# Reordering inside a slot of an attention stage: the score maxima, GpSimd's half of a remainder, and two small edits of the first slots

## The chip, the cores and the metric

The kernel runs on one core of a Trainium2 chip. The metric is the device time of one execution in microseconds; the median of several runs is compared. The engines are TensorE (PE in the rows), VectorE (DVE), ScalarE (ACT) and GpSimd (POOL); SyncE (SP) issues the DMAs. Each engine works through its own queue of instructions in the order in which they are written, and they meet at semaphores.

## The reference

```python
# x (4, 2048, 512), ctx (4, 77, 512); Wq, Wo (512, 512); 16 heads of 32
xn = layernorm(x)
Q, K, V = split(xn @ Wq.T), split(ctx @ Wq.T), split(ctx @ Wq.T)
attn = softmax(Q @ K.T / sqrt(32))
x = x + merge(attn @ V) @ Wo.T
# feed-forward, activations and weights fake-quantized to int8
xq = fake_quant(layernorm(x), clip_x)
h = fake_quant(silu(xq @ qw(w_gate).T) * (xq @ qw(w_up).T), clip_down)
x = x + h @ qw(w_down).T
```

All tensors are float32. The attention part needs accuracy beyond one reduced-precision product, so most operands are kept as a high part and a remainder (hi + lo), and products are made of three terms.

## The kernel before, in words

The kernel has three stages: `attend` (to about 600 us of the span), `expand` and `contract`. The change touches only `attend`.

`attend` treats the 8192 tokens in 16 blocks of 512. A block has 4 groups of 128 feature columns (4 heads each), and one group of one block is an item: 64 items, n = 0 to 63, with `n.block = n // 4` and `n.g = n % 4`. The work is pipelined over slots k = -9 to 72. In each slot every engine handles parts of several items, and `at(k, lag)` is item k + lag. Each engine has its own `for k in SLOTS` loop; the order in which its parts are written is the order in which it executes them.

TensorE in slot k, before: scores of item k-2 (L937, with the negated maxima added by L941), denominators and attention times V of item k-3 (L888, L893, L897, L901), in slots with k % 4 == 1 a transposition of the maxima (L860), the q product of item k+4 (L961: 12 matmuls, 8 with the high part of x and 4 with its remainder), the maxima's scores of item k+3 (`maximum`, L874: 4 matmuls into the same PSUM banks `S` that the scores use), and last the output projection of item k-7 (`project`, L918, 12 matmuls). The order of waits matters here: `maximum(n)` waits for the exponentials of item n-5 and the reduction of item n-1, the scores of item k-2 for the reduction of item k+2 (`maxed`), and `project(n)` for `aT_l` of all four items of n's block, and it waits for the fourth of them already at the first item of the block.

ScalarE in slot k: exponentials of item k-2 (L569), the fp16 cast of both halves of the probabilities (L573 for `HA`, L575 for `HB`; before item 7 the first is done by VectorE at L728), logarithm and reciprocal of the denominators of item k-3 (L586, L588), the high part of x (L594), the high part of q of item k+4 (L616), a weight's int8 code (L632), and last the high part of the attention output of item k-3 into `aT` (L636), once VectorE has written `att`.

VectorE in slot k: statistics of a token tile (L680, L681), moments of the finished rows of item k-8 (L691 to L693), measuring of a weight (L646; L652 and L653 when a row of it is finished), the remainder of half `HA` of the probabilities of item k-2 (L730, `pl_a`), the scaling of q of item k+4 (L738), the reduction of the maxima's scores of item k+3 (L745), `att` of item k-3 (L752, into one buffer, so that it waits for `aT_l` of the item before), and the sum with x of item k-7 (L791).

GpSimd in slot k, before: the remainder of x (L489), the remainder of the attention output of item k-4 (L494, `aT_l`), the remainder of q (L498), the half `HB` of the remainder of the probabilities of item k-2 (L504, `pl_b`; it waits for VectorE's half of the same item), then small parts: K's remainder in slot -1 (L508), spreading K over the head mask for the next batch (L481), Wo's remainder (L519), a weight's cast (L529), and the factors of layernorm (L535 to L539).

Of the kernel before, what the change touches and what calls it, by code (L numbers as in the profile page):

```python
# [24 lines left out]
F32 = mybir.dt.float32  # L25
# [151 lines left out]
EXP_BITS, V_BITS = 11, 12  # L177
EARLY, LATE = 7, 60
V_SLOTS = (2, 3, 4, 6)
SQ = 32  # L180
STAT_LAGS = ((9, 0, TT), (8, TT, 2 * TT), (9, 2 * TT, 3 * TT), (11, 3 * TT, STEPS))

# [28 lines left out]
def attend(nc, x_t, x_k, ctxT, WqT, WoT, clip_x, clip_down, w_gate, w_up, w_down, ident, headmask, negsel,  # L211
# [8 lines left out]
    with ExitStack() as st:  # L220
# [94 lines left out]
        def at(k, lag):  # L315

            return Item(k + lag) if 0 <= k + lag < STEPS else None
# [44 lines left out]
        with nc.Block() as block:  # L362
# [108 lines left out]
            @block.gpsimd  # L471
            def _(pool):
                own = Chain(pool, own_p)
                nc.gpsimd.memset(allones[:], 1.0).then_inc(consts, 1)
                nc.gpsimd.memset(epsb[:], EPS).then_inc(consts, 1)
                nc.gpsimd.memset(mx[:], 0.0).then_inc(mx_zero, 1)
                nc.gpsimd.memset(ones[:], 1.0).then_inc(consts, 1)
                nc.gpsimd.memset(ebias[:], EXP_BITS * math.log(2.0)).then_inc(consts, 1)
                def spread_k(b, j):

                    nc.gpsimd.tensor_scalar(kbd[:, b % 2, :, j], kt[:, b, 0].bitcast(F32), hmask[:, j:j + 1], None,  # L481
                                            ALU.mult).then_inc(kbd_rdy, 1)

                for k in SLOTS:
                    for n in [n for n in (at(k, 8), at(k, 7)) if n and (n.block < 2) == (n.n == k + 8)]:
                        if n.n == 2:
                            pool.wait_ge(rs_rdy, 1)
                        pool.wait_ge(xT_h, n.n + 1)
                        nc.gpsimd.tensor_tensor(xT[:, n.par, 1, n.g], xt32[:, n.n % RINGX], xT[:, n.par, 0, n.g].bitcast(F32),  # L489
                                                ALU.subtract).then_inc(xT_l, 1)  # L490
                    if (n := at(k, -4)) and n.n < STEPS - 1:

                        pool.wait_ge(aT_h, n.n + 1)
                        nc.gpsimd.tensor_tensor(aT[:, n.par, 1, n.g], att[:], aT[:, n.par, 0, n.g].bitcast(F32),  # L494
                                                ALU.subtract).then_inc(aT_l, 1)
                    for n in [n for n in (at(k, 4), at(k, 3)) if n and (n.n <= 5) == (n.n == k + 4)]:
                        pool.wait_ge(qT_h, n.n + 1)
                        nc.gpsimd.tensor_tensor(qT[:, n.ring, 1], q32[:, n.n % 2], qT[:, n.ring, 0].bitcast(F32), ALU.subtract).then_inc(qT_l, 1)  # L498
                    if (n := at(k, -2)) and n.n < LATE:

                        pool.wait_ge(ph_b, n.n + 1)
                        pool.wait_ge(pl_a, n.n + 1)
                        after(pool, valued, n.n)
                        nc.gpsimd.tensor_tensor(pl[:, HB], pr[:, HB], ph[:, HB], ALU.subtract).then_inc(pl_b, 1)  # L504
                    if k == -1:
                        pool.wait_ge(k32_rdy, 1)
                        for g in range(GROUPS):
                            nc.gpsimd.tensor_tensor(kt[:, :, 1, g], k32[:, g].rearrange("p (b k) -> p b k", b=BATCH),  # L508
                                                    kt[:, :, 0, g].bitcast(F32), ALU.subtract).then_inc(k_lo, 1)
                    if k == -5:  # L510
                        pool.wait_ge(c_in, 16)
                        nc.gpsimd.tensor_copy(negw[:], neg[:].unsqueeze(2).to_broadcast([P, GROUPS, KEYS])).then_inc(consts, 1)
                        pool.wait_ge(mask_in, 16)
                        pool.wait_ge(k_hi, GROUPS)
                        for j in range(HG):
                            spread_k(0, j)
                    if 0 <= k < KT:
                        pool.wait_ge(wo_hi, k + 1)
                        nc.gpsimd.tensor_tensor(wo[:, 1, k], wo32[:, k], wo[:, 0, k].bitcast(F32), ALU.subtract).then_inc(wo_lo, 1)  # L519
                    b, j = k // PER + 1, k % PER - 4  # L520
                    if 0 <= j < HG and 1 <= b < BATCH:
                        after(pool, m_scored, PER * (b - 1))
                        spread_k(b, j)
                    if k == 8:
                        nc.gpsimd.tensor_copy(id16[:], id32[:])
                    if (w := weight(k - W_FIRST - 2)) and w.coded:
                        pool.wait_ge(w_coded, w.code + 1)
                        after(pool, w_turned[w.ring], 16 * (w.code // 2), 1 << 30)
                        nc.gpsimd.tensor_copy(wb[:, w.ring, 0:w.width], wc[:, w.ring, 0:w.width]).then_inc(w_cast, 1)  # L529
                    for n in measured_at(k):  # L530
                        if n.g == TT - 1 and n.block > 2:

                            pool.wait_ge(r0_rdy, n.block + 1)
                            pool.wait_ge(rs_rdy, n.block)
                            own.step(nc.gpsimd.tensor_scalar(rv[:], mv[:, n.par, :, 1], EPS, None, ALU.add))  # L535
                            own.step(nc.gpsimd.tensor_tensor(rt[:], r0[:], r0[:], ALU.mult))
                            own.step(nc.gpsimd.tensor_tensor(rt[:], rv[:], rt[:], ALU.mult))
                            own.step(nc.gpsimd.tensor_scalar(rt[:], rt[:], -0.5, 1.5, ALU.mult, ALU.add))
                            nc.gpsimd.tensor_tensor(rs[:, 0:TT], rt[:], r0[:], ALU.mult).then_inc(rt_rdy, 1)  # L539
# [99 lines left out]
            def _(dve):  # L639
                own = Chain(dve, own_d)  # L640
                def measure(w):
# [5 lines left out]
                    if w.last:  # L647
# [4 lines left out]
                        own.step(nc.vector.tensor_scalar(sc, wmax[:, col], 1.0 / QMAX, None, ALU.mult))  # L652
                        nc.vector.reciprocal(winv[:, col], sc).then_inc(w_scaled, 1)  # L653

                for k in SLOTS:
                    if k == FIRST:

# [66 lines left out]
                    if (n := at(k, -2)):  # L724
# [3 lines left out]
                            nc.vector.tensor_copy(ph[:, HA], pr[:, HA]).then_inc(ph_a, 1)  # L728
                        dve.wait_ge(ph_a, n.n + 1)
                        nc.vector.tensor_tensor(pl[:, HA], pr[:, HA], ph[:, HA], ALU.subtract).then_inc(pl_a, 1)  # L730
                    if (n := at(k, 4)):
                        dve.wait_ge(q_done, n.n + 1)
                        after(dve, qT_l, n.n - 1)
                        if n.n in (0, TT):
                            dve.wait_ge(rsb_rdy, n.block + 1)
                        if n.block > 1:
                            dve.wait_ge(rsb_in[n.par], 16 * (n.block // 2))
                        nc.vector.tensor_tensor(q32[:, n.n % 2], q_bank(n.n)[:], rsb[:, n.par], ALU.mult).then_inc(q_scaled, 1)  # L738
                    if (n := at(k, 3)):

                        dve.wait_ge(m_scored, n.n + 1)
                        if n.n == 0:
                            dve.wait_ge(mx_zero, 1)
                        after(dve, m_turned, n.block)
                        nc.vector.tensor_reduce(mx5[:, :, :, n.g], S[:, :, 0:HG * KEYS].rearrange("p t (h k) -> p t h k", h=HG),  # L745
                                                AX.X, ALU.max).then_inc(maxed, 1)
                    done = at(k, -3)
                    if done:
                        dve.wait_ge(rcp_rdy, done.n + 1)
# [45 lines left out]
            def _(pe):  # L795
# [127 lines left out]
                for k in SLOTS:  # L923
# [24 lines left out]
                    if (n := at(k, 4)):  # L948

                        pe.wait_ge(xT_h, GROUPS * (n.block + 1))  # L950
                        after(pe, q_scaled, Q_FREE[n.n] if n.n < len(Q_FREE) else n.n)
                        if n.n == 0:
                            pe.wait_ge(wc_hi, 2)
                        ins = 0
                        for wp, xp in ((0, 0), (1, 0), (0, 1)):
                            if n.n == 0 and wp == 1:
                                pe.wait_ge(wc_lo, 2)
                            if xp == 1:
                                pe.wait_ge(xT_l, GROUPS * (n.block + 1))
                            for j in range(KT):  # L960
                                mm = nc.tensor.matmul(q_bank(n.n)[:], wq[:, wp, j, P * n.g:P * (n.g + 1)], xT[:, n.par, xp, j],  # L961
                                                      start=(ins == 0), stop=(ins == 3 * KT - 1))
                                ins += 1
                        mm.then_inc(q_done, 1)
                    if k == 0:
                        turn_rs(1)
                    if k % 4 == 1 and (n := at(k, -1)) and n.block == 0:
                        turn_maxima(n)
                    if at(k, 4):
                        maximum(at(k, 3))  # L970
                    if k in V_SLOTS:
                        project_v(V_SLOTS.index(k))
# [485 lines left out]
```

## Time and profile before

| | us |
|---|---|
| median of 3 runs | 1084.98 (1084.82 to 1087.05) |
| profiled execution, its own time | 1086.07 |
| its span | 1083.8 |
| TensorE matmul busy | 1049.3 (97%) |
| VectorE busy | 857.0 (79%) |
| ScalarE busy | 752.1 (69%) |
| GpSimd busy | 532.3 (49%) |

The busy time is over the whole span, so it mixes three stages with different limits. GpSimd has most of its work in `attend`. Matmuls are pipelined, and a busy TensorE isn't one at its peak.

### The profile page before, as it was taken

The numbers are of one execution on the slowest core, as the hardware profiler recorded it, in microseconds if no ns is written. First come the engines' busy times: TensorE is split into PE (matmuls) and PEld (weight loads), VectorE is DVE, ScalarE is ACT, GpSimd is POOL, SyncE is SP. The second block draws the span as 40 slices with busy tenths as digits, with TensorE's granted clock in tenths as the row PEclk, the third lists the DMA queues.
The fourth block names the chain that finished last, engine by engine and source line by source line (L and its number), as shares of the span: only waits on it lengthen the run. The fifth ranks groups of instructions, "written<-read, shape, count | busy, mean of one in ns | idle before, by whom it ended". The sixth has DMA issues, their size and how long they took to land. (4 is left out here: it accounts for less than half of the span.)

```text
span 1083.8 us, 18315 instructions
## 1 busy us (share of the span) xinstructions
PE 1049.3 (97%) x6391; PEld 617.6 (57%) x6421; DVE 857.0 (79%) x1426; ACT 752.1 (69%) x905; POOL 532.3 (49%) x445
## 2 busy tenths in 40 slices
PE   8779999999999999999998899999999999999998
PEld 6646666767776667777754544444444444344444
DVE  5888989899888898777767778777777877777576
ACT  4577888888888888888777375666657564875550
POOL 5878877798777887677552000000000000386485
PEclk9989999999999999999999999999999999999999
DMA  7434667667655555652147356767673313899995
GB/s 248 137 98 122 186 186 186 194 184 207 172 164 175 169 176 159 189 152 74 68 153 231 108 205 223 253 213 262 214 245 96 112 25 97 343 415 426 425 398 223
DMA packets 121609, 214.40 MB, mean 198 GB/s; under 512 B 59056, under 2 KB 68144, under 8 KB 110384
## 3 DMA queue, kind: packets, MB, share of 16 engines
q1 hardware_dynamic: 118640, 184.41, 52.9%
q10 hardware_dynamic: 2880, 28.84, 6.4%
q8 instruction: 52, 0.85, 0.3%
q14 instruction: 37, 0.30, 0.1%
HBM read 134.26 MB, written 66.75 MB: 185 GB/s over the span
## 5 line engine op out<-in xcount | busy, mean ns | idle before, releaser
L1324 POOL TENSOR_TENSOR x<-x,c_y 128x512 f32<-128x512 f32 x32 | 53.8, 1714 | 365.9 <-DVE c_y L1368 348.6
L1096 ACT ACTIVATE e_sg<-e_G,x_gus 128x512 f32<-128x512 f32 x176 | 119.1, 685 | 114.5 <-PE e_G L1208 110.7
L961 PE MATMUL a_Q<-a_xT,wq 128*128 128x512 f32 x732 | 186.4, 403 | 1.2 <-DVE wq L663 1.2
L1168 DVE SCALAR_TENSOR_TENSOR h<-e_U,x_gus,e_sg 128x512 f32<-128x512 f32 x176 | 131.9, 749 | 69.8 <-PE e_U L1212 40.8
L504 POOL TENSOR_TENSOR a_pl<-a_pr,a_ph 77x1024 f16<-77x1024 f32 x60 | 129.0, 2150 | 113.4 <-DVE a_pl L730 73.7
L1208 PE MATMUL e_G<-e_cT,gu 128*128 128x512 bf16 x690 | 178.8, 379 | 0.7
L1212 PE MATMUL e_U<-e_cT,gu 128*128 128x512 bf16 x689 | 178.6, 379 | 0.7
L918 PE MATMUL a_O<-a_wo,a_aT 128*128 128x512 f32 x720 | 176.8, 395 | 0.6 <-POOL a_aT L494 0.6
L961 PEld LDWEIGHTS a_Q<-a_xT,wq 128*128 128x128 f32 x732 | 134.0, 190 | 47.6 <-issue 19.1
L569 ACT ACTIVATE a_pr<-a_S,a_ebias 77x2048 f32<-77x2048 f32 x64 | 125.9, 1967 | 45.3 <-PE a_S L941 43.6
L918 PEld LDWEIGHTS a_O<-a_wo,a_aT 128*128 128x128 f32 x720 | 133.4, 189 | 28.8 <-issue 3.3
L1431 PE MATMUL c_Y<-dn,gu 128*128 128x512 bf16 x649 | 140.4, 379 | 0.6 <-DVE gu L1359 0.6
L730 DVE TENSOR_TENSOR a_pl<-a_pr,a_ph 77x1024 f16<-77x1024 f32 x64 | 92.6, 1447 | 53.1 <-ACT a_ph L573 52.8
L1344 ACT ACTIVATE c_c<-h,h_inv 128x3072 int8<-128x3072 f32 (+4 forms) x36 | 83.5, 2373 | 48.8 <-DVE gu L1359 43.2
L1208 PEld LDWEIGHTS e_G<-e_cT,gu 128*128 128x128 bf16 x704 | 68.9, 98 | 83.3 <-issue 0.4
L1212 PEld LDWEIGHTS e_U<-e_cT,gu 128*128 128x128 bf16 x704 | 68.9, 98 | 82.9
L1151 DVE TENSOR_REDUCE hmax<-h 128x1 f32<-128x512 f32 x160 | 108.0, 676 | 0.0
L1431 PEld LDWEIGHTS c_Y<-dn,gu 128*128 128x128 bf16 x649 | 63.3, 98 | 77.6 <-DVE gu L1359 1.5
L494 POOL TENSOR_TENSOR a_aT<-a_att,a_aT 128x512 fp32r<-128x512 f32 x63 | 83.1, 1319 | 25.0 <-ACT a_aT L636 24.9
L745 DVE TENSOR_REDUCE a_mx<-a_S 128x16 f32<-128x1232 f32 x64 | 91.4, 1428 | 1.4 <-PE a_S L874 1.4
L489 POOL TENSOR_TENSOR a_xT<-a_xt,a_xT 128x512 fp32r<-128x512 f32 x64 | 84.5, 1322 | 11.9 <-ACT a_xT L594 11.3
L498 POOL TENSOR_TENSOR a_qT<-a_q,a_qT 128x512 fp32r<-128x512 f32 x64 | 87.1, 1362 | 3.5 <-ACT a_qT L616 3.5
(188 smaller groups left out, 1547.7 us busy)
## 6 DMA issues: line engine op xcount, KB each, us to landing
x<-x_d SPq DMA_DIRECT2D x24, 1024.0 KB, 6.3
h_d<-h SPq DMA_DIRECT2D x20, 1024.0 KB, 4.1
a_xr<-in_x SPq DMA_DIRECT2D x64, 256.0 KB, 3.5
a_xt<-in_xT SPq DMA_DIRECT2D x64, 256.0 KB, 3.8
x_d<-a_xr SPq DMA_DIRECT2D x64, 256.0 KB, 2.5
a_xs<-in_x SPq DMA_DIRECT2D x60, 256.0 KB, 3.8
h<-h_d ACTq DMA_DIRECT2D x10, 1536.0 KB, 24.5
h<-h_d ACTq DMA_DIRECT2D x10, 1280.0 KB, 27.7
```

Source lines behind the costliest of these rows:

```text
L504: nc.gpsimd.tensor_tensor(pl[:, HB], pr[:, HB], ph[:, HB], ALU.subtract).then_inc(pl_b, 1)
L569: nc.scalar.activation(pr[:], S[0:KEYS], ACT.Exp, scale=SM_SCALE, bias=ebias[:, 0:1]).then_inc(exped, 1)
L730: nc.vector.tensor_tensor(pl[:, HA], pr[:, HA], ph[:, HA], ALU.subtract).then_inc(pl_a, 1)
L745: nc.vector.tensor_reduce(mx5[:, :, :, n.g], S[:, :, 0:HG * KEYS].rearrange("p t (h k) -> p t h k", h=HG), AX.X, ALU.max).then_inc(maxed, 1)
L918: mm = nc.tensor.matmul(projection(n), aT[:, n.par, ap, j, P * n.g:P * (n.g + 1)], wo[:, wp, j], start=(ins == 0), stop=(ins == 3 * KT - 1))
L961: mm = nc.tensor.matmul(q_bank(n.n)[:], wq[:, wp, j, P * n.g:P * (n.g + 1)], xT[:, n.par, xp, j], start=(ins == 0), stop=(ins == 3 * KT - 1))
L1096: nc.scalar.activation(sg[:, s], G[:, t % GU], ACT.Silu, scale=gus[:, t:t + 1]).then_inc(silued, 1)
L1151: nc.vector.tensor_reduce(hm[:, p, t:t + 1], h[:, place(b // 2, p), t], AX.X, ALU.max, apply_absolute_value=True)
L1168: nc.vector.scalar_tensor_tensor(out=h[:, place(u, p), t], in0=U[:, t % GU], scalar=gus[:, IT + t:IT + t + 1], in1=sg[:, s], op0=ALU.mult, ...
L1208: mm = nc.tensor.matmul(G[:, t % GU], gu[:, t, k], cT[:, p, k], start=(k == 0), stop=(k == KT - 1))
L1212: mm = nc.tensor.matmul(U[:, t % GU], gu[:, IT + t, k], cT[:, p, k], start=(k == 0), stop=(k == KT - 1))
L1431: mm = nc.tensor.matmul(Y[:, TT * (k % 2) + t], cb[:, k % 2, j, P * t:P * (t + 1)], dn[:, :, j], start=(j == 0), stop=(j == IT - 1))
```

## The change

Four edits, all in `attend`:

1. TensorE issues `maximum(at(k, 3))` inside the q product, after its first 8 matmuls (ahead of the 4 with the remainder of x), instead of after all 12.
2. VectorE reduces the maxima of item k+3 before it scales q of item k+4.
3. GpSimd's half of the remainder of the probabilities (`half`) comes ahead of the remainders of the attention output (`low_a`) and of q (`low_q`), in all slots before the 60th.
4. In slot -1 GpSimd waits for the factors of block 1 (`rs_rdy` 2) before K's remainder; and the spreading of K for the next batch is in slots 8 to 11 of each 16 instead of 4 to 7.

```diff
+SPLIT_UNTIL = 60
@@ gpsimd
+                def half(k):
+                    if (n := at(k, -2)) and n.n < LATE:
+                        pool.wait_ge(ph_b, n.n + 1)
+                        pool.wait_ge(pl_a, n.n + 1)
+                        after(pool, valued, n.n)
+                        nc.gpsimd.tensor_tensor(pl[:, HB], pr[:, HB], ph[:, HB], ALU.subtract).then_inc(pl_b, 1)
+                def low_a(k):
+                    if (n := at(k, -4)) and n.n < STEPS - 1:
+                        pool.wait_ge(aT_h, n.n + 1)
+                        nc.gpsimd.tensor_tensor(aT[:, n.par, 1, n.g], att[:], aT[:, n.par, 0, n.g].bitcast(F32),
+                                                ALU.subtract).then_inc(aT_l, 1)
+                def low_q(k):
+                    for n in [n for n in (at(k, 4), at(k, 3)) if n and (n.n <= 5) == (n.n == k + 4)]:
+                        pool.wait_ge(qT_h, n.n + 1)
+                        nc.gpsimd.tensor_tensor(qT[:, n.ring, 1], q32[:, n.n % 2], qT[:, n.ring, 0].bitcast(F32), ALU.subtract).then_inc(qT_l, 1)
...
-                    (the same three parts in line, in the order low_a, low_q, half)
+                    for part in (half, low_a, low_q) if k < SPLIT_UNTIL else (low_a, low_q, half):
+                        part(k)
                     if k == -1:
+                        pool.wait_ge(rs_rdy, 2)
                         pool.wait_ge(k32_rdy, 1)
...
-                    b, j = k // PER + 1, k % PER - 4
+                    b, j = k // PER + 1, k % PER - 8
@@ vector
+                def scale_q(k):          (the former part for at(k, 4), unchanged)
+                def reduce_maxima(k):    (the former part for at(k, 3), unchanged)
...
+                    for part in (reduce_maxima, scale_q) if k < SPLIT_UNTIL else (scale_q, reduce_maxima):
+                        part(k)
@@ tensor
                             if xp == 1:
+                                if k < SPLIT_UNTIL:
+                                    maximum(at(k, 3))
                                 pe.wait_ge(xT_l, GROUPS * (n.block + 1))
...
-                    if at(k, 4):
+                    if at(k, 4) and k >= SPLIT_UNTIL:
                         maximum(at(k, 3))
```

## Rows read from the trace of the kernel before

**Rows 1.** Busy us (and count) of each engine in one stretch; granted clock, DMA share, GB/s.

```profile
core 0: us, PE busy (x) PEld busy (x) DVE busy (x) ACT busy (x) POOL busy (x), PEclk, DMA share, GB/s
300.00:350.00 50.00, 50.00 (x382) 34.93 (x379) 41.41 (x78) 41.53 (x53) 36.18 (x32) 1.00 0.58 176
```

**Rows 2.** TensorE's longest wait: line, what was waited for, us in total, times, longest.

```profile
PE a_S L937 <- DVE a_mx L745: 13.0, 7, 3.0
```

**Rows 3.** Order of time (start, us, engine, line, operation): denominators of slots 7, 31, 35, 60.

```profile
92.18 0.62 PE L888 MATMUL a_DN<-a_ph,a_ones 77*32 77x512 f16 x4
...
300.93 0.40 PE L888 MATMUL a_DN<-a_ph,a_ones 77*32 77x512 f16 x4
...
335.55 0.40 PE L888 MATMUL a_DN<-a_ph,a_ones 77*32 77x512 f16 x4
...
551.87 0.40 PE L888 MATMUL a_DN<-a_ph,a_ones 77*32 77x512 f16 x4
```

**Rows 4.** Order of time, slots 31 and 32: ScalarE, VectorE and GpSimd.

```profile
301.06 1.97 ACT L569 ACTIVATE a_pr<-a_S,a_ebias 77x2048 f32<-77x2048 f32 x1 [0.93 <-PE a_S L941]
...
303.06 1.06 ACT L573 ACTIVATE a_ph<-a_pr 77x1024 f16<-77x1024 f32 x1
...
304.21 1.22 DVE L730 TENSOR_TENSOR a_pl<-a_pr,a_ph 77x1024 f16<-77x1024 f32 x1 [1.35 <-ACT a_ph L573]
...
305.57 2.16 POOL L504 TENSOR_TENSOR a_pl<-a_pr,a_ph 77x1024 f16<-77x1024 f32 x1 [2.69 <-DVE a_pl L730]
...
307.31 0.74 DVE L752 SCALAR_TENSOR_TENSOR a_att<-a_A,a_sv,a_lnd 128x512 f32<-128x512 f32 x1
307.68 0.60 POOL L529 CAST w_b<-w_c 128x512 bf16<-128x512 int8 x1
308.07 0.63 ACT L636 ACTIVATE a_aT<-a_att 128x512 fp32r<-128x512 f32 x1 [0.21 <-DVE a_att L752]
...
309.51 1.27 POOL L494 TENSOR_TENSOR a_aT<-a_att,a_aT 128x512 fp32r<-128x512 f32 x1
...
309.65 1.97 ACT L569 ACTIVATE a_pr<-a_S,a_ebias 77x2048 f32<-77x2048 f32 x1 [0.94 <-PE a_S L941]
```

**Rows 5.** Order of time, slot 8: VectorE between `att` and the probabilities' halves.

```profile
100.48 0.69 DVE L791 CUSTOM_DVE_ANT_0 a_xr<-a_O,a_xr 128x512 f32<-128x512 f32 x1 [0.51 <-issue]
...
104.26 1.30 DVE L728 CAST a_ph<-a_pr 77x1024 f16<-77x1024 f32 x1
```

**Rows 6.** Order of time, slots 31 and 32: TensorE.

```profile
305.58 2.92 PE L918 MATMUL a_O<-a_wo,a_aT 128*128 128x512 f32 x12
...
309.75 0.60 PE L893 MATMUL a_A<-a_ph,a_v 77*32 77x512 f16 x8
...
310.71 3.01 PE L961 MATMUL a_Q<-a_xT,wq 128*128 128x512 f32 x12
...
313.57 0.73 PE L874 MATMUL a_S<-a_kbd,a_qT 128*128 128x308 f32 x4
...
314.13 2.93 PE L918 MATMUL a_O<-a_wo,a_aT 128*128 128x512 f32 x12
```

**Rows 7.** Order of time, then stretches of 10 us (PEclk third from the right).

```profile
62.28 1.05 PE L937 MATMUL a_S<-a_qT,a_kt 32*77 32x512 f32 x12 [3.01 <-DVE a_mx L745]
...
81.32 0.92 PE L937 MATMUL a_S<-a_qT,a_kt 32*77 32x512 f32 x12 [2.20 <-DVE a_mx L745]
...
90.25 1.57 PE L937 MATMUL a_S<-a_qT,a_kt 32*77 32x512 f32 x12 [2.60 <-DVE a_mx L745]
...
60.00:70.00 10.00, 7.72 (x46) 4.38 (x47) 7.18 (x9) 6.79 (x10) 8.37 (x6) 0.66 0.56 184
...
90.00:100.00 10.00, 9.75 (x63) 6.43 (x64) 8.69 (x13) 7.20 (x10) 8.79 (x8) 0.83 0.24 67
```

**Rows 8.** Order of time, slots -1 and 0: VectorE's factors of block 1, and TensorE.

```profile
34.33 0.87 DVE L773 TENSOR_TENSOR a_rt<-a_r 128x4 f32<-128x4 f32 x1
...
37.68 0.62 PE L846 MATMUL a_A<-id,a_rs 128*128 128x128 f32 x4 [2.27 <-DVE a_rs L778]
```

More of the change, by code:

```diff
@@ L490, in _ @@
                                                 ALU.subtract).then_inc(xT_l, 1)
[L491 to L504, printed above, removed]
+                    for part in (half, low_a, low_q) if k < SPLIT_UNTIL else (low_a, low_q, half):
+                        part(k)
                     if k == -1:
+                        pool.wait_ge(rs_rdy, 2)
                         pool.wait_ge(k32_rdy, 1)
@@ L653, in measure, with scale_q, reduce_maxima @@
                         nc.vector.reciprocal(winv[:, col], sc).then_inc(w_scaled, 1)
+                def scale_q(k):
+                    if (n := at(k, 4)):
+                        dve.wait_ge(q_done, n.n + 1)
+                        after(dve, qT_l, n.n - 1)
+                        if n.n in (0, TT):
+                            dve.wait_ge(rsb_rdy, n.block + 1)
+                        if n.block > 1:
+                            dve.wait_ge(rsb_in[n.par], 16 * (n.block // 2))
+                        nc.vector.tensor_tensor(q32[:, n.n % 2], q_bank(n.n)[:], rsb[:, n.par], ALU.mult).then_inc(q_scaled, 1)
+                def reduce_maxima(k):
+                    if (n := at(k, 3)):
+                        dve.wait_ge(m_scored, n.n + 1)
+                        if n.n == 0:
+                            dve.wait_ge(mx_zero, 1)
+                        after(dve, m_turned, n.block)
+                        nc.vector.tensor_reduce(mx5[:, :, :, n.g], S[:, :, 0:HG * KEYS].rearrange("p t (h k) -> p t h k", h=HG),
+                                                AX.X, ALU.max).then_inc(maxed, 1)
                 for k in SLOTS:
@@ L730, in _ @@
                         nc.vector.tensor_tensor(pl[:, HA], pr[:, HA], ph[:, HA], ALU.subtract).then_inc(pl_a, 1)
[L731 to L746, printed above, removed]
+                    for part in (reduce_maxima, scale_q) if k < SPLIT_UNTIL else (scale_q, reduce_maxima):
+                        part(k)
                     done = at(k, -3)
```

## The prediction

> **What bounds the kernel now.** I read the busy time by stretch first, then who waited for whom on TensorE, then one slot in order of time. In the attention stage TensorE is busy throughout [rows 1]: 50.00 of 50 us in the middle of it. The waits say the same: its largest is 13.0 us in 7 places, the scores of L937 waiting for VectorE's maxima [rows 2]. All seven lie outside the steady part, in slots 2 to 7 and 61. From the start of the denominators (L888) in slot 7 to those of slot 60 the stage takes 551.87 - 92.18 = 459.7 us for 53 slots; four steady slots take 335.55 - 300.93 = 34.62 us, so 8.66 us each [rows 3]. A steady slot is as long as TensorE's own stream of matmuls, and the other engines stand beside it with slack. The question is therefore whether the new order leaves that slack or makes a ring of waits that is longer than 8.66 us.
>
> **The new ring.** Take slot 31, which begins with the exponentials (L569) at 301.06; the order of time gives each step by the distance of two starts [rows 4]. Exponentials to ScalarE's first cast (L573): 2.00. To VectorE's first half of the remainder (L730): 1.15. To GpSimd's half (L504), which waits for VectorE's (pl_a): 1.36. GpSimd's half to its next instruction: 2.11. In the kernel before, these 6.62 us end in nothing urgent, for the remainder of the attention output (`low_a`, L494) has been done ahead of them: in slot 32 it starts at 309.51, before that slot's exponentials (309.65), while the half comes 4.51 us after them (305.57 - 301.06).
>
> Now the half stands ahead of `low_a` in GpSimd's queue, and `low_a`(k-4) of slot k is what two others wait for in the same slot. One is VectorE's L752, att(k-3): it overwrites `att`, so it waits for aT_l >= k-3. The other is TensorE's project(k-7), when k-7 is the first item of a block: it waits for aT_l of all four items, and the fourth is item k-4.
>
> *Every slot.* 6.62 for the steps above; then `low_a` 1.27; an estimated 0.10 to hand over (0.14 lies between the end of L730, 304.21 + 1.22, and the start of L504); L752 to ScalarE's copy into aT (L636) 0.76; and that copy, 0.63, which is ahead of the next slot's exponentials on the same in-order queue, so 0.60 with the overlap of two activations. The sum is 9.35 us from one L569 to the next. TensorE isn't in it. Its own 8.66 fits inside, and it then waits each slot for L752 (att_rdy) ahead of L893. The bounds of an ordinary slot are 8.66 (everything hidden) and 9.35 + 0.2 (each handover at its largest).
>
> *Slots with VectorE's full weight measuring.* After L752 comes VectorE's queue up to the next pl_a: L752 0.74, then L791 to L728 in slot 8, 104.26 - 100.48 = 3.78 [rows 5], 0.10 to the next. From there 1.36 + 2.11 + 1.27 + 0.10 back to L752: 9.46 us. This decides where the row of a weight is finished: slots 8 to 26, 29, 35, 41 and 47.
>
> *Slots k = 7, 11, ..., 59, the first item of a block.* Exponentials to the end of `low_a`: 6.62 + 1.27 = 7.89, and 0.10 to TensorE. From the start of project (L918, 305.58) to the next exponentials (309.65) is 4.07 us of work in TensorE's order [rows 4, 6]: project, then the next scores. So 12.06 us a slot. TensorE would have come to project earlier: from L893 (309.75) to project (314.13) is 4.38 us, and L893 goes as soon as L752 is done, about 0.5 us ahead of the exponentials. It arrives 3.9 us after them and idles 4.1 us.
>
> *The sum at full clock.* 53 slots from 7 on: 14 of 12.06 (168.8), 17 of 9.46 (160.8), 22 of 9.35 (205.7), together 535.3 against 459.7: +75.6 us.
>
> **The clock.** After waits of 3.01 and 2.60 us the granted clock fell to its lower level, 1.2 GHz; after 2.20 it stayed at 2.4 [rows 7]. The mean granted clock of the two stretches is 0.66 and 0.83 over 10 us: 3.4 and 1.7 us of full-speed work were lost. An idle of 4.1 us is longer than all these, so I count a fall in each of the 14 slots, and because project and scores, which are on the ring, come right behind the idle, its price is paid in full. I take 1.7 (the shorter case, since TensorE works without a break from there on): 14 x 1.7 = +23.8. The bounds are 0 and 14 x 3.4 = 47.6.
> The Trainium skill (TensorE: Matmul & The Clock Gate, "What's actually happening") says that the throttled clock is the default and that activity alone lifts it. By that rule the idle in front of project is charged twice, once as waiting and once as slow matmuls; the two falls in the trace agree with it.
>
> **Maxima inside the q product, and reduced ahead of the scaling of q.** TensorE's work is the same. The q product, the maxima and project follow each other at 2.86 and 0.56 us with no gap between the three [rows 6], so splitting 12 matmuls into 8 and 4 costs nothing that I can see (bounds: -0.1 to +0.3 us a slot, and it would be hidden in the ring's slack). The maxima need exponentials that end 1.97 after their start (311.62 in slot 32), while the ninth matmul of the q product would be due at about 310.71 + 8/12 x 2.86 = 312.6: 1.0 us of margin. The reduction (1.43 us) comes some 1.6 us sooner: 0.92 from TensorE, 0.68 from VectorE. That pays only where TensorE waited for it [rows 2]. Slots 2, 3 and 4 had 5.6 us of them; from slot 4 on the new ring takes over. The scaling of q comes 1.5 us later, and so does ScalarE's copy of it. That copy must be done before L636, which now waits for 8.7 us of the ring anyway, so: nothing.
>
> **Block 1's factors ahead of K's parts.** GpSimd now waits for VectorE's tiny rs chain before it subtracts K's parts. One of the chain's operations on 4 columns took 0.87 us beside GpSimd, and TensorE then waited 2.27 us for it (L846) [rows 8]. I count 2.2 back. Behind the waiting GpSimd stand K's four parts, not needed until the scores at 45.7.
> The Trainium skill (SBUF - State Buffer, "SBUF: two separate sides") has VectorE and GpSimd take one pair of ports by an exclusive lock held for a whole instruction. By it this edit, and a half that follows VectorE's, are both right, and the change should gain; but the time that the lock costs in steady slots lies off TensorE's stream, and the lock says nothing of the queue behind the half.
>
> **kbd's spreading four slots later** (GpSimd, 1.05 us each) leaves slots 4 to 7 and is done by slot 11 of each 16; its reader comes in slot 13. Nothing either way. No DMA is moved.
>
> Slots before 7 together: 2.2 back from the factors, some 2 to 3 of the 5.6 from the maxima, near nothing from slots 4 to 6 (38.1 us for the four from 3 to 7 before, and the ring holds them to 9 or more). I take -5, between -14 (all the waits) and 0. From slot 60 on GpSimd's order is the old one.
>
> **Sum.** +75.6 + 23.8 - 5 = +94. The profiled execution took 1086.07 us (span 1083.8); the median of the runs is 1084.98, 1.1 lower. 1085 + 94 = 1179 us.
>
> **The rivals.**
> *The clock holds, or falls in a few slots only.* For it: 2.20 us didn't drop it. Against: both longer waits did. 1085 + 75.6 - 5 = 1156.
> *Long falls.* As in the stretch of 0.66, 3.4 us each: 1203. This is also what the clock rule above gives if the short idles in ordinary slots (some 0.7 us each) keep activity down.
> *Only project's wait is real*, and ordinary slots stay at 8.66, because some step of my ring is shorter than I read it: 14 x (12.06 - 8.66 + 1.7) - 5 = +66, 1151. Against it: the ring would have to be 0.7 us shorter, and every segment but two handovers is a measured distance.
> *Faster.* The half first is harmless, since low_a's two readers are late enough; then what is left is the waits recovered, 11.5 without slot 61 [rows 2] and 2.27 [rows 8]: 1071. It decides if `low_a` ends before 305.58 in a slot like 31, and for that the half would have to start 3.4 us sooner than its pl_a allows. The lock rule speaks for this side, the queue order against it.
>
> **How the numbers follow.** Forecast 0.56; clock holds 0.16; long falls 0.12; only project's wait 0.11; faster 0.04, of no effect 0.01. The range 1145 to 1207 holds the first four with a few us of error in the early slots. A measurement of this kernel can tell about 0.2% from no change. Faster 0.04, within 0.2% 0.01, slower 0.95.
>
> **What would show it.** Right: L888's starts 9.3 to 9.5 us apart in ordinary slots and 12 to 14 in slots 7, 11, ...; TensorE waiting some 4 us for GpSimd's L494 ahead of L918, 14 times; L752 idle before it and released by L494; the exponentials released by ScalarE's own L636, or idle for nothing; granted clock under 1 in most 10 us stretches; L745 gone from TensorE's waits but for slot 61. Wrong: slots of 8.6 us in the middle, or L494 not among the releasers of L918 and L752.

## The result: 9.7% slower, and the profile after

The changed kernel takes 1191.81 us (median of 4 runs, 1190.43 to 1193.21), the kernel before 1086.01 in the same comparison; the ratio is 1.097 (95% interval 1.0952 to 1.0988), +105.8 us. The prediction was 1179, range 1145 to 1207. The profiled execution took 1191.62 us, its span is 1189.7.

TensorE's waits in the profile after (line, what was waited for, us in total, times, longest) have two new rows on top; they answer to [rows 2]:

```profile
PE a_O L939 <- POOL a_aT L499: 53.6, 15, 4.2
PE a_A L914 <- DVE a_att L773: 13.7, 19, 1.6
PE a_S L958 <- DVE a_mx L687: 7.5, 7, 1.6
```

L939 is project (L918 before), L499 is `low_a` (L494), L773 writes `att` (L752), L958 are the scores (L937), L687 is the reduction (L745). All 15 waits are those of a block's first item: 13 of them, in slots 11 to 59, are 4.0 to 4.2 us long, the one of slot 7 is 0.43 and the one of slot 63 is 0.63. The reduction is still waited for in the same 7 places, for 7.5 us instead of 13.0. VectorE's waits say the same of `att`:

```profile
DVE a_att L773 <- POOL a_aT L499: 93.0, 55, 2.1
```

The ring in order of time (start, us, engine, line, operation, idle before and releaser), slot 36 with the start of slot 37, answers to [rows 4]:

```profile
404.13 1.97 ACT L582 ACTIVATE a_pr<-a_S,a_ebias 77x2048 f32<-77x2048 f32 x1 [5.44 <-PE a_S L962]
...
406.12 1.06 ACT L586 ACTIVATE a_ph<-a_pr 77x1024 f16<-77x1024 f32 x1
...
407.29 1.22 DVE L765 TENSOR_TENSOR a_pl<-a_pr,a_ph 77x1024 f16<-77x1024 f32 x1 [1.48 <-ACT a_ph L586]
...
408.64 2.15 POOL L492 TENSOR_TENSOR a_pl<-a_pr,a_ph 77x1024 f16<-77x1024 f32 x1 [9.03 <-DVE a_pl L765]
...
410.76 1.28 POOL L499 TENSOR_TENSOR a_aT<-a_att,a_aT 128x512 fp32r<-128x512 f32 x1
...
412.17 0.75 DVE L773 SCALAR_TENSOR_TENSOR a_att<-a_A,a_sv,a_lnd 128x512 f32<-128x512 f32 x1 [1.72 <-POOL a_aT L499]
...
412.96 0.63 ACT L649 ACTIVATE a_aT<-a_att 128x512 fp32r<-128x512 f32 x1 [1.16 <-DVE a_att L773]
...
413.50 1.95 ACT L582 ACTIVATE a_pr<-a_S,a_ebias 77x2048 f32<-77x2048 f32 x1
```

Each row starts where the one above it ends, plus a handover, and the last is the first again: 413.50 - 404.13 = 9.37 us. The second exponentials show no idle at all, because ScalarE went straight on from its copy into aT; nothing in that row names TensorE. GpSimd waits 9.03 us ahead of its half in this slot, with `low_a` ready behind it.

A slot of a block's first item, slot 35, is longer. TensorE's project:

```profile
389.25 1.95 ACT L582 ACTIVATE a_pr<-a_S,a_ebias 77x2048 f32<-77x2048 f32 x1
...
395.88 1.26 POOL L499 TENSOR_TENSOR a_aT<-a_att,a_aT 128x512 fp32r<-128x512 f32 x1
...
397.39 5.46 PE L939 MATMUL a_O<-a_wo,a_aT 128*128 128x512 f32 x12 [4.08 <-POOL a_aT L499]
```

From 389.25 to project are 8.14 us. From project to the exponentials of slot 36 (404.13) are 6.74, where [rows 4, 6] had 4.07; the 12 matmuls took 5.46 us instead of 2.92. The granted clock (third number from the right) in stretches of 1 us shows why:

```profile
396.00:397.00 1.00, 0.00 (x0) 0.65 0.02 6
...
400.00:401.00 1.00, 1.00 (x4) 0.50 0.00 0
401.00:402.00 1.00, 1.00 (x4) 0.50 0.00 0
402.00:403.00 1.00, 1.00 (x7) 0.50 0.00 0
403.00:404.00 1.00, 1.00 (x16) 0.94 0.00 0
```

0.50 is 1.2 GHz. The level fell within the idle, about 1 us before project, and came back just before the exponentials. In slot 39 it is low for about half as long, and all of that lies in project:

```profile
440.00:441.00 1.00, 0.70 (x3) 0.83 0.00 0
441.00:442.00 1.00, 1.00 (x4) 0.50 0.00 0
...
443.00:444.00 1.00, 1.00 (x4) 0.50 0.00 0
444.00:445.00 1.00, 1.00 (x8) 0.96 0.00 0
```

Slot 35 took 14.88 us and slot 39 took 13.81. The longer stretch answers to [rows 1]:

```profile
300.00:350.00 50.00, 44.48 (x314) 29.72 (x313) 33.72 (x66) 33.77 (x43) 33.12 (x29) 0.93 0.53 153
```

### The profile page after: what moved, and what is told of

Read it like the earlier page. It is cut to its first block and busy times, and to the rows that moved or that the text cites. A ratio compares the mean times of both kernels' runs of the same rounds, so it can differ in the third digit from the quotient of the medians.

```text
span 1189.7 us, 18316 instructions
## 1 busy us (share of the span) xinstructions
PE 1092.0 (92%) x6391; PEld 635.1 (53%) x6421; DVE 839.2 (71%) x1426; ACT 753.0 (63%) x905; POOL 526.9 (44%) x445
## 5 line engine op out<-in xcount | busy, mean ns | idle before, releaser
L939 PE MATMUL a_O<-a_wo,a_aT 128*128 128x512 f32 x720 | 203.8, 439 | 55.2 <-POOL a_aT L499 53.6
L492 POOL TENSOR_TENSOR a_pl<-a_pr,a_ph 77x1024 f16<-77x1024 f32 x60 | 128.5, 2142 | 228.0 <-DVE a_pl L765 194.2
L939 PEld LDWEIGHTS a_O<-a_wo,a_aT 128*128 128x128 f32 x720 | 151.3, 214 | 102.1 <-issue 68.7
L984 PE MATMUL a_Q<-a_xT,wq 128*128 128x512 f32 x732 | 199.9, 409 | 0.4 <-DVE wq L698 0.4
L773 DVE SCALAR_TENSOR_TENSOR a_att<-a_A,a_sv,a_lnd 128x512 f32<-128x512 f32 x64 | 48.0, 749 | 94.3 <-POOL a_aT L499 93.0
L765 DVE TENSOR_TENSOR a_pl<-a_pr,a_ph 77x1024 f16<-77x1024 f32 x64 | 80.3, 1254 | 40.3 <-ACT a_ph L586 40.0
L687 DVE TENSOR_REDUCE a_mx<-a_S 128x16 f32<-128x1232 f32 x64 | 91.7, 1433 | 10.9 <-PE a_S L895 9.4
L499 POOL TENSOR_TENSOR a_aT<-a_att,a_aT 128x512 fp32r<-128x512 f32 x63 | 82.7, 1312 | 20.7 <-ACT a_aT L649 20.7
L649 ACT ACTIVATE a_aT<-a_att 128x512 fp32r<-128x512 f32 x64 | 40.5, 633 | 79.0 <-DVE a_att L773 78.8
```

The costliest lines, as they stand in the source:

```text
L939: mm = nc.tensor.matmul(projection(n), aT[:, n.par, ap, j, P * n.g:P * (n.g + 1)], wo[:, wp, j], start=(ins == 0), stop=(ins == 3 * KT - 1))
```

## The experiments

Twelve kernels; each ratio is to runs of the kernel before on the same chip. The theory: all of the loss is the half standing ahead of `low_a` in GpSimd's queue, and it has three parts: a ring through `att` in ordinary slots, project's wait at a block's first item, and the clock that falls in that wait. The main rivals: the maxima's new place costs TensorE time, or one part returns what another loses.

**The old order of GpSimd's parts, the rest as changed.**

```diff
-for part in (half, low_a, low_q) if k < SPLIT_UNTIL else (low_a, low_q, half):
+for part in (low_a, low_q, half):
```

> The changed kernel with GpSimd's parts back in their old order in all slots; maxima inside the q product, the reduction first, the factors' wait and kbd's later slots stay. My theory (all of the slowdown is the half standing ahead of low_a): ordinary slots and first-item slots back to 8.55 and 8.9 us, TensorE waits for L499 nearly gone, 1080 to 1085 us, that is 0 to 6 under the kernel before. Rival (the maxima's place or the reduction ahead of the scaling of q costs time too): over 1090 us, with slots above 8.66 in the middle.

Measured: 1084.79 us, ratio 0.9976 (0.9967 to 0.9986). The whole loss is gone with one line. The maxima's new place isn't where it comes from: 1080 to 1085 had been expected, and over 1090 if it were.

**Only the order of GpSimd's parts, the rest as before.** The kernel before with `(half, low_a, low_q)` below slot 60.

> The kernel before with nothing but the half ahead of the two remainders in slots below 60. My theory: the whole loss and a little more, since the gains of the first slots are missing: 1190 to 1198 us, ring of 9.36 us in ordinary slots, 13.8 to 14.8 in slots 7, 11, ... Rival (the loss needs the later maxima or the later scaling of q as well): below 1170.

Measured: 1191.37 us, ratio 1.0955 (1.0936 to 1.0974). That line alone is the whole loss; the other edits bring nothing beside it (1191.81 with all of them).

**low_a, half, low_q.**

```diff
-(half, low_a, low_q) if k < SPLIT_UNTIL
+(low_a, half, low_q) if k < SPLIT_UNTIL
```

> The changed kernel with GpSimd's order low_a, half, low_q: the half ahead of q's remainder only. My theory (low_a behind the half is the whole cause; low_q has slots of slack): within 2 us of e1_old_pool_order, 1080 to 1086. Rival (what costs is that GpSimd holds all its work until VectorE's half is there): well over 1100.

Measured: 1085.00 us, ratio 0.9978 (0.9968 to 0.9988). That is the time of the first run: the half may stand ahead of q's remainder, only `low_a` must not be behind it. It isn't free in every slot, for slot 11 takes 10.35 us between denominators instead of 8.55 (two runs below come back to it). That GpSimd holds everything behind the half until VectorE's half is there costs nothing visible here; but its waits for it are 75.3 us in all and 4.3 at most, against 194.2 and 9.0 in the changed kernel, so waits that long aren't tested by this run.

**TensorE's idle filled.** In slots of a block's first item, ahead of the wait for `aT_l`:

```diff
+if n.g == 0 and n.block < 14:
+    for _ in range(17):
+        nc.tensor.matmul(O[:], wo[:, 0, 0, 0:P], wo[:, 0, 1], start=True, stop=True)
 after(pe, aT_l, n.n - n.g + 4)
```

> The changed kernel with 17 matmuls (128x128 by 512, about 3.9 us at full clock) that do nothing needed, written to the projection's bank, between TensorE's arrival at project of a block's first item and its wait for low_a; project overwrites them. My theory (a first-item slot is 12.06 us of ring and 2.3 us of lost clock): granted clock 1.0 through the stage, first-item slots 12.0 to 12.2 us, 14 x 2.3 = 32 us less than the changed kernel, about 1160. Rival (the slots are long because the ring is longer than 12.06, and the clock costs nothing): no change from 1192, with the clock at 1.0.

Measured: 1166.42 us, ratio 1.0725 (1.0707 to 1.0744), 0.0245 of 1087 or 26.6 us less than the changed kernel, where 32 had been expected. Slot 7 gained nothing (11.78 us against 11.80), for TensorE waited there only 0.43 us; the other 13 went from 14.25 to 12.12 on average, 2.1 us each. The same stretch as above now has

```profile
300.00:350.00 50.00, 49.17 (x337) 34.19 (x340) 33.68 (x64) 33.73 (x45) 32.66 (x28) 1.00 0.50 138
```

that is, a granted clock of 1.00. The first-item slot 35 in order of time:

```profile
377.80 1.96 ACT L583 ACTIVATE a_pr<-a_S,a_ebias 77x2048 f32<-77x2048 f32 x1
...
381.48 3.84 PEld L938 LDWEIGHTS a_O<-a_wo 128*128 128x128 f32 x17
...
385.81 3.01 PE L943 MATMUL a_O<-a_wo,a_aT 128*128 128x512 f32 x12
...
389.97 1.97 ACT L583 ACTIVATE a_pr<-a_S,a_ebias 77x2048 f32<-77x2048 f32 x1 [2.66 <-PE a_S L966]
```

389.97 - 377.80 = 12.17 us at full clock, where 12.06 was worked out; the 13 slots took 12.11 to 12.17. More work on TensorE, and a faster kernel, because it stood in time that was idle.

**Two buffers for att.** att(k-3) then waits for `low_a`(k-5) instead of `low_a`(k-4).

```diff
-after(dve, aT_l, done.n)
+after(dve, aT_l, done.n - 1)       # att -> att2[:, done.n % 2]; RINGQ 7 -> 6
```

> The changed kernel with att in two buffers, so that att(k-3) waits for low_a(k-5) and no longer for low_a(k-4) (for room, q's ring has 6 places instead of 7). My theory (two separate costs: the ring through att in ordinary slots, and project's wait at a block's first item): ordinary slots back to 8.55 and 8.93, first-item slots still some 14.3 us, total about 1085 + 14 x 5.7 - 1 = 1164. Rival (one ring only: without att's wait the first-item slots get shorter as well): below 1150. Rival (att's wait isn't what makes ordinary slots 9.36): 1190.

Measured: 1165.99 us, ratio 1.0739 (1.0705 to 1.0773). Ordinary slots are 8.55 us again, slots with the maxima's transposition 8.93, and the first row of TensorE's waits stays:

```profile
PE a_O L939 <- POOL a_aT L499: 52.2, 15, 5.0
```

The wait of L914 for `att` is no longer among the long ones. So the ordinary slots' loss was the single buffer. The four executions lie further apart than elsewhere (1162.44 to 1171.56).

The first-item slots took 12.2 to 14.9 us between exponentials. The two short ones are 19 and 31. TensorE idled there as long as in most others, and its clock didn't fall:

```profile
219.54 3.00 PE L939 MATMUL a_O<-a_wo,a_aT 128*128 128x512 f32 x12 [3.42 <-POOL a_aT L499]
...
210.00:230.00 20.00, 16.58 (x126) 1.00 0.67 176
```

In slot 35, after a wait of 3.45 us, the clock fell and the slot took 13.83. So the length of the wait alone doesn't decide whether the clock falls; in the changed kernel it fell at all 13 waits of 4.0 to 4.2 us.

**Both: two buffers and the filler.**

> Two buffers for att as above, and the 17 filling matmuls ahead of project of a block's first item. My theory (the terms add up): 14 x (12.06 - 8.6) = 48 us over the kernel before less the 1 to 2 of the first slots, about 1132. Rival (removing one lets another take its place): above 1145.

Measured: 1140.12 us, ratio 1.0497 (1.0483 to 1.0511), 8 us over the expected sum. Between denominators the first-item slots are 12.4 us where 12.06 was expected, three of them 13.3 to 13.9 (7, 11 and 27). In the other 11 the 17 matmuls are more than the idle: `low_a` ends at 371.27 in slot 35, and project starts when the filler ends, at 371.73. That is some 4 us of the miss. The rest is in the three slots; in 11 and 27 `low_a` itself started 0.6 us later after the exponentials, and project waited 0.9 us for it. TensorE's waits for `low_a` are 2.4 us in 3 places.

**The old order in every fourth slot.**

```diff
-if k < SPLIT_UNTIL
+if k < SPLIT_UNTIL and k % 4 != 3
```

> The changed kernel with GpSimd's old order in the slots of a block's first item (k % 4 == 3) alone; the half is ahead in the other three. My theory: project's wait and the lost clock are gone, the ring of 9.36 us stays in ordinary slots, 39 x 0.7 = 27 us: about 1111. Rival (the first-item slots give the others back their time, as TensorE runs ahead): about 1090.

Measured: 1113.68 us, ratio 1.025 (1.0234 to 1.0266). This is the ring by itself, 27 us, as worked out; TensorE's waits for `low_a` ahead of project aren't in the list any more, those of L914 for `att` are 17.9 us in 27 places. Between exponentials the 39 ordinary slots are 28.9 us longer than before, and only 2.8 of them come back in the 14 fourth ones.

**A version meant to be faster than both.** low_a, half, low_q below slot 11 and the old order from there; in slot 60 `maximum(at(k, 3))` ahead of `project(at(k, -7))`.

> Maxima inside the q product and reduced first, the factors' wait and kbd's later slots as changed; GpSimd low_a, half, low_q in slots below 11 and the old order from there; in slot 60 the maxima of item 63 ahead of project. My theory: the run with low_a, half, low_q throughout gains 3 us to slot 11, loses 1.8 there and 1.5 in slot 61; both go: 3 us less, about 0.995 of the kernel before. Rival (what is won early is lost at the end of the stage, where ScalarE bounds): 0.998.

Measured: 1084.70 us, ratio 0.9983 (0.9974 to 0.9992), where 0.995 had been expected. TensorE still waits in slot 11:

```profile
128.87 1.61 DVE L765 TENSOR_TENSOR a_pl<-a_pr,a_ph 77x1024 f16<-77x1024 f32 x1 [0.46 <-ACT a_ph L586]
129.37 2.25 POOL L499 TENSOR_TENSOR a_aT<-a_att,a_aT 128x512 fp32r<-128x512 f32 x1
...
131.87 1.40 PE L939 MATMUL a_O<-a_wo,a_aT 128*128 128x512 f32 x5 [1.56 <-POOL a_aT L499]
```

`low_a` fell together with VectorE's half, and both took longer than their usual 1.28 and 1.22 us; project paid for it.

**The same with the old order from slot 8 on.** `k < 11` became `k < 8`.

> As e8_best_of_both, but GpSimd's order low_a, half, low_q ends with slot 7 instead of slot 10, so that q's remainder is out of GpSimd's way before kbd's parts come in slots 8 to 11. My theory (the 1.6 us that TensorE waits for low_a in slot 11 comes from GpSimd being late there, its low_a falling together with VectorE's half): slot 11 back to 8.56 us, 1.8 us less, 0.9965 of the kernel before. Rival (VectorE's half falls on low_a there whatever the order): slot 11 stays at 10.4, 0.998.

Measured: 1083.46 us, ratio 0.9961 (0.9949 to 0.9974). Slot 11 is 8.56 us again, as expected. `low_a` now ends before VectorE's half gets in its way, and the collision falls on `low_q`, for which nobody is waiting:

```profile
128.38 1.29 POOL L499 TENSOR_TENSOR a_aT<-a_att,a_aT 128x512 fp32r<-128x512 f32 x1
129.16 1.60 DVE L765 TENSOR_TENSOR a_pl<-a_pr,a_ph 77x1024 f16<-77x1024 f32 x1 [0.47 <-ACT a_ph L586]
129.63 2.28 POOL L506 TENSOR_TENSOR a_qT<-a_q,a_qT 128x512 fp32r<-128x512 f32 x1
130.13 2.91 PE L939 MATMUL a_O<-a_wo,a_aT 128*128 128x512 f32 x12
```

**Only the maxima and their reduction.**

> The kernel before with the maxima inside the q product and the reduction ahead of the scaling of q, in slots below 60, and nothing else. My theory (it pays only where TensorE waited for the reduction, in slots 2 to 7, and there another wait takes over part of it): slots from 8 on unchanged, 0 to 2 us less than before, 0.998 to 1.000. Rival (a split q product costs TensorE something in each slot): slots of 8.6 to 8.7 us, slower by 3 us or more.

Measured: 1088.18 us, ratio 1.0009 (0.9999 to 1.0018): no gain, and no cost per slot either (8.55 and 8.93 us between denominators from slot 10 on, but for one slot of 9.77). TensorE's waits for the reduction are 10.2 us in 6 places instead of 13.0 in 7, but other waits came up in the first slots: `maximum` now stands ahead of a third of a q product, so that its own waits delay matmuls that could have run. One of them:

```profile
25.43 0.84 PE L894 MATMUL a_S<-a_kbd,a_qT 128*128 128x308 f32 x4 [1.53 <-POOL a_kbd L482]
```

The kernel before had 0.6 us there.

**Only the factors' wait and kbd's later slots.**

> The kernel before with GpSimd's wait for block 1's factors ahead of K's parts and kbd's parts four slots later, and nothing else. My theory: TensorE's wait for the factors (2.3 us before) goes, and half of it comes back as a wait for the reduction of the maxima; 1 to 2 us less, 0.998 to 0.999. Rival (K's parts are then late): equal or slower.

Measured: 1082.85 us, ratio 0.996 (0.9946 to 0.9974): 4 us less, where 1 to 2 had been expected. In the profile TensorE still waits 2.2 us for the factors (2.3 before), but something else holds them there. VectorE waited for a transfer ahead of them:

```profile
32.74 0.69 DVE L715 BATCH_NORM_STATS2 a_bst<-a_xs 128x6 f32<-128x512 f32 x1 [1.58 <-DMA a_xs<-in_x]
```

and began the factors at 36.31 instead of 34.33. The profiled execution took 1085.08 us, 2.2 over the median (the six lie between 1081.22 and 1085.12), so it doesn't show where 4 us went.

**The factors' wait, kbd's slots and the early half together, with TensorE's and VectorE's old order.** As the version above with `k < 8`, without the maxima inside the q product and without the reduction first.

> The kernel before with the factors' wait, kbd's later slots, GpSimd's order low_a, half, low_q in slots below 8, and in slot 60 the maxima of item 63 ahead of project; TensorE's and VectorE's order is the old one. My theory (the maxima inside the q product bring nothing, the other edits each a little and in different slots): 1 to 2 us less than with the factors and kbd alone, 0.994 to 0.995. Rival (they share one gain in the first slots, so that it counts once): 0.996.

Measured: 1080.61 us, ratio 0.9937 (0.9922 to 0.9952), the fastest of all: 6.3 us under the median of the kernel before, a little more than expected. Its interval overlaps the one of the factors and kbd alone. Up to slot 1 both kernels issue the same work; here no transfer held VectorE up, and TensorE's wait for the factors is short:

```profile
36.09 0.62 PE L867 MATMUL a_A<-id,a_rs 128*128 128x128 f32 x4 [0.63 <-DVE a_rs L799]
```

That is 1.6 us earlier than before (37.68 in [rows 8]), so the wait that GpSimd was given does what it was meant to do.

## Why the prediction was right, point by point

**The ring.** Right in its place and its size. The 22 ordinary slots took 9.34 to 9.38 us between exponentials, 9.36 on average, where 9.35 had been added up from rows of before [rows 4]. The old order in every fourth slot gives its price alone, 27 us. One sign was named wrongly: L888's starts were to be 9.3 to 9.5 us apart and 12 to 14 in slots 7, 11, ... The denominators (L909 now) are 8.5 to 10.1 and 14.1 to 16.4 apart: TensorE runs ahead in the ordinary slots and stops at a block's first item. It is the exponentials that show the ring.

**Slots with VectorE's measuring.** 9.46 was forecast and 9.52 measured for the 17, but that the two are close is luck: 12 of them took 9.34 to 9.46, two 9.52 and 9.58, and three 9.96 to 10.15. VectorE's queue wasn't the bound that I made it in most, and why three slots are so long isn't shown.

**First-item slots.** Project's wait was forecast at 4.1 us, 14 times. It is 4.08 in slot 35 and 4.0 to 4.2 in 13 slots; in slot 7 it is 0.43. The filler shows the parts: 12.17 us at full clock in a slot (12.06 forecast), and 2.1 us of clock.

**The clock.** This is the term that was too small. I took 1.7 us for each fall, which is what the shorter of the two falls of before had cost [rows 7]. Slots 11 to 59 took either 13.6 to 13.9 us (seven of them) or 14.5 to 15.0 (six), mostly by turns, so 1.7 and 2.7 over 12.1. The stretches of 1 us above show the two kinds: in slot 39 the level is low from about 440.7 to 444.1, in slot 35 from about 396.3 to 403.1, and the first 1.1 us of that lie in the idle; 5.7 us of work at half speed cost some 2.8. So six of the falls were of the kind that the rival with long falls had priced at 3.4. The 14 slots with their 14.07 on average cost 4 us more than forecast (slot 7 took 11.80: there the clock was low ahead of project, and only the wait got shorter). The filler shows that it is the idle: with that filled the granted clock is 1.00. The Trainium skill (TensorE: Matmul & The Clock Gate, "What's actually happening"), by which activity releases the throttle, agrees with this run: matmuls that nobody needed kept the clock up. The sign "granted clock under 1 in most 10 us stretches" didn't come: 17 of the 56 stretches between 100 and 660 us are under 1.

**The first slots.** -5 was forecast, and nothing was gained. The exponentials of slot 7 start at

```profile
92.30 1.97 ACT L569 ACTIVATE a_pr<-a_S,a_ebias 77x2048 f32<-77x2048 f32 x1 [0.78 <-PE a_S L941]
```

before and at

```profile
92.94 1.95 ACT L582 ACTIVATE a_pr<-a_S,a_ebias 77x2048 f32<-77x2048 f32 x1
```

after, 0.6 us later. (Slot 7's denominators come 1.7 us earlier, 90.50 against 92.18 in [rows 3], but only because they stand at another place of the ring.) The step that failed is the sum "2.2 back from the factors, some 2 to 3 from the maxima". VectorE did finish the factors 1.1 us sooner, at 36.29 instead of 37.42, and TensorE no longer waits for them, but it arrives late itself:

```profile
36.72 0.70 DVE L778 TENSOR_TENSOR a_rs<-a_rt,a_r 128x4 f32<-128x4 f32 x1
```

```profile
36.13 0.16 DVE L799 TENSOR_TENSOR a_rs<-a_rt,a_r 128x4 f32<-128x4 f32 x1
...
38.01 0.60 PE L867 MATMUL a_A<-id,a_rs 128*128 128x128 f32 x4
```

Its transposition of them starts at 38.01 against 37.68 [rows 8]; with the maxima's new place alone it starts at 38.09, without a wait. The maxima gave back 5.5 us of TensorE's waits for the reduction, but others took their place: 3.7 us for `att` in slots 5 to 7 and 1.5 for kbd (0.6 before). The forecast that L745 would be gone from the list but for slot 61 was wrong: all seven waits are still there, shorter on the whole.

**The sum.** From slot 7 to slot 60 the exponentials are 657.68 - 92.94 = 564.7 us apart against 459.7 before: +105.0, where +99.4 was forecast. Of the 5.6 too little, the 14 slots make 4.4 and the 17 slots 1.0. With the +0.6 in front of it that is +105.7, all of the measured difference; the rest of the kernel didn't move. The forecast was 11.4 us short of it, half from the slots and half from the gain in the first ones, and both misses go the same way. The measured time lies about midway between the forecast (1179) and the rival with long falls (1203).

**The rivals.** "The clock holds" is refuted by the 1 us stretches. "Only project's wait" is refuted by ordinary slots of 9.36 us, and by the run with two buffers, which had to remove the ring to bring them back to 8.55. "Faster" failed where it was said to be decided: `low_a` ends at 397.14 in slot 35, 4 us after TensorE's arrival.

Left open: what exactly gives the 4 us of the factors and kbd's slots. They weren't run apart. In its profile slot 7's denominators start 2.9 us earlier (89.29 instead of 92.18), but slot 7 then takes 11.35 us instead of 9.28, most of it in a q product of 4.74 us at the lower clock, and 0.8 us are left in slot 8. The executions of this kernel and of the fastest one differ in their mean granted clock too (0.990 to 0.995 and 0.992 to 0.997, the quickest at the highest), so part of the gain may be a shorter time at the lower level in the first slots; no run separates the two. Also open is what decides whether an idle brings a fall at all, and a short or a long one. In the kernel before a wait of 2.20 us brought none, and the one of 2.27 [rows 8] did (the clock is low from 39.0 to 42.5), which the prediction left out.

## What to carry to other kernels

Before an instruction that waits is moved forward in an in-order queue, list what stands behind it and who waits for that in the same iteration: here a step with 4.5 us of dependencies was put ahead of one that had been ready all along. Follow every such wait until it closes, and add the distances of starts from the trace; if the ring is longer than the bounding engine's slot, it is the new period, whatever the engine's busy share. An idle of some 4 us of TensorE has to be priced with the slow matmuls behind it, here 1.7 or 2.7 us more each time. And where a wait is removed, look at what the engine meets next: here waits for `att` and kbd took the place of those for the reduction.

## What the runs showed of the hardware

A tiny VectorE operation can be held for as long as a run of GpSimd instructions lasts. With the order changed alone, the first operation of the factors (4 columns) took 3.85 us beside GpSimd's four K parts; in the profile after, where it comes ahead of them, the same operation (L794) takes 0.15:

```profile
34.11 3.85 DVE L793 TENSOR_TENSOR a_rt<-a_r 128x4 f32<-128x4 f32 x1
34.90 3.04 POOL L520 TENSOR_TENSOR a_kt<-p_k,a_kt 128x308 fp32r<-128x308 f32 x4
```

```profile
35.55 0.15 DVE L794 TENSOR_TENSOR a_rt<-a_r 128x4 f32<-128x4 f32 x1
```

It isn't always so. In the kernel before, beside the same four parts, each operation of the chain took the time of about one GpSimd instruction (0.87 us for the first in [rows 8], then 0.70, 0.72 and 0.70):

```profile
35.09 3.05 POOL L508 TENSOR_TENSOR a_kt<-p_k,a_kt 128x308 fp32r<-128x308 f32 x4
35.23 0.70 DVE L774 SCALAR_TENSOR_TENSOR a_rt<-a_mv,a_rt 128x4 f32<-128x4 f32 x1
```

The Trainium skill (SBUF - State Buffer, "SBUF: two separate sides") says that GpSimd and a VectorE instruction with two SBUF inputs, as the first of the factors is, hold a shared pair of ports for a whole instruction and that the other is blocked, not slowed. The rows of the kernel before agree, one GpSimd instruction for each of VectorE's. The row of 3.85 us agrees in that VectorE got through when GpSimd's run of four had ended, at 37.94; why it didn't get in between two of the four, as it did before, isn't shown.
